# Tokens laid over partitions by chunk in a two-layer recurrent, attention and expert kernel

## The reference

```python
xn = layernorm(x)
# layer 0: a recurrence over 16 states, gated, and a small per-feature network
u = LN(xn)@Ws.T + bs + LN(xn)@Wi.T + bi
h_t = tanh(h_{t-1} @ A.T + u_t)                    # over the 2048 tokens
s = (H@Wo.T + bo) * sigmoid(LN(xn)@Wg.T + bg) + xn
t = xn@Win + bin_
g = einsum(relu(t[..., None]*W1 + b1), W2) + b2; g = g@Wout + bout
x = x + s * silu(g)
xn = layernorm(x)
# layer 1: attention over the first axis (the 4 sequences), 16 heads, causal, softmax with 1 + sum
q, k, v = xn@Wq.T + bq, xn@Wk.T + bk, xn@Wv.T + bv
s = attention_one(q, k, v)                         # 4 x 4 scores per token and head
# 8 experts, 2 per token, 2048 places per expert, given out in token order
logits = xn.reshape(8192, 256)@wg
topv, topi = top_k(softmax(logits), 2)
pos = cumsum(one_hot(topi.T)) - 1                  # places; a token past the last place is dropped
g = sum over the 2 of gate * (relu(xn@w1[e] + b1[e])@w2[e] + b2[e])
x = x + s * silu(g)
```

## Time and profile before

| | us |
|---|---|
| median of three runs | 1446.29 (1444.0 to 1450.97) |
| the profiled execution | 1449.93, of which the span in the trace is 1448.0 |
| PE busy | 1192.6 (82%) |
| DVE busy | 1016.9 (70%) |
| ACT busy | 639.6 (44%) |
| POOL busy | 624.9 (43%) |

### The profile page before, as it was taken

One profiled execution on the slowest core, in us unless ns is written; L12 is line 12 of the kernel. 1 busy time (PEld: TensorE's weight loads), 2 busy tenths in 40 slices (PEclk: granted clock), 3 DMA queues, 4 the chain that ended last, 5 costly groups with the idle time before them and its releaser, 6 DMA issues. The chain is left out here.

```text
span 1448.0 us, 23203 instructions
## 1 busy us (share of the span) xinstructions
PE 1192.6 (82%) x7551; PEld 809.2 (56%) x7551; DVE 1016.9 (70%) x1925; ACT 639.6 (44%) x981; POOL 624.9 (43%) x530
## 2 busy tenths in 40 slices
PE   4899999588888886244999989999999998999910
PEld 3566666366666665032665656766666666666610
DVE  7756667658888888595666776676676765776638
ACT  4855555234444432004446354454454454553522
POOL 6500000137777777203545545545445445464430
PEclk9999999699999999556999999999999999999965
DMA  9250000000000010103546445554446545465469
GB/s 323 98 194 1 1 0 1 15 30 30 30 30 30 30 31 16 59 4 103 114 73 130 82 89 115 102 100 82 101 95 111 107 66 121 83 108 106 63 160 344
DMA packets 165458, 122.35 MB, mean 85 GB/s; under 512 B 88528, under 2 KB 158032, under 8 KB 165232
## 3 DMA queue, kind: packets, MB, share of 16 engines
q1 hardware_dynamic: 131424, 83.90, 20.0%
q0 software_dynamic: 25200, 35.85, 16.1%
q10 hardware_dynamic: 8736, 1.33, 0.5%
HBM read 58.91 MB, written 44.30 MB: 71 GB/s over the span
## 5 line engine op out<-in xcount | busy, mean ns | idle before, releaser
L1721 ACT ACTIVATE e_h_all<-e_pH,e_b1c,e_h_scale 128x512 f32<-128x512 f32 x256 | 199.8, 780 | 285.7 <-PE e_pH L1762 262.6
L1776 PE MATMUL e_pY<-e_w_hi,e_h_hi 128*128 128x256 f16 x1024 | 279.6, 273 | 20.4 <-DVE e_w_lo L1596 11.1
L1505 POOL DMA_INDIRECT e_xg<-xn_rows,e_icol x140 | 161.9, 1157 | 284.1 <-DVE e_icol L1537 251.3
L1778 PE MATMUL e_pY<-e_w_hi,e_h_lo 128*128 128x256 f16 x1024 | 279.1, 273 | 0.0
L1777 PE MATMUL e_pY<-e_w_lo,e_h_hi 128*128 128x256 f16 x1024 | 279.1, 273 | 0.0
L1520 POOL DMA_INDIRECT expert_sums<-e_yo,e_dcol x128 | 213.2, 1665 | 81.1 <-issue 43.8
L1639 DVE TENSOR_TENSOR e_h_lo<-e_h_all,e_h_hi 128x512 f16<-128x512 f32 x256 | 177.5, 693 | 62.6 <-ACT e_h_hi L1721 56.4
L1760 PE MATMUL e_pH<-e_xT,e_w_hi 128*128 128x512 f16 x512 | 196.0, 383 | 22.5 <-DMA e_xT<-e_xs 15.4
L1761 PE MATMUL e_pH<-e_xT,e_w_hi 128*128 128x512 f16 x512 | 195.8, 382 | 0.0
L1762 PE MATMUL e_pH<-e_xT,e_w_lo 128*128 128x512 f16 x512 | 195.6, 382 | 0.0
L1776 PEld LDWEIGHTS e_pY<-e_w_hi,e_h_hi 128*128 128x128 f16 x1024 | 100.1, 98 | 46.7 <-DVE e_h_lo L1639 28.1
(11 more groups left out here) (245 smaller groups left out, 2195.5 us busy)
## 6 DMA issues: line engine op xcount, KB each, us to landing
raw<-expert_w SPq DMA_DIRECT2D x18, 1024.0 KB
expert_sums<-a_zero SPq DMA_DIRECT2D x10, 1024.0 KB, 10.7
x_st<-x SPq DMA_DIRECT2D x16, 512.0 KB, 8.9
xn_rows<-c_xn SPq DMA_DIRECT2D x16, 512.0 KB, 3.0
f_ya<-expert_sums SPq DMA_DIRECT2D x16, 512.0 KB, 6.8
out<-f_ya SPq DMA_DIRECT2D x16, 512.0 KB, 5.8
e_xg<-xn_rows,e_icol POOLq DMA_INDIRECT x140
e_xT<-e_xs SPq DMA_TRANSPOSE x136
```

The source lines that it names most:

```text
L1505: pool.indirect_dma_start(xg[:, q, 0:D + E], None, v.xn3_dram, bass.IndirectOffsetOnAxis(icol[u][:, q:q + 1], axis=0), bounds_check=N - 1, ...
L1721: last = act.activation(dst, pH[h % NPH][:, :], ACT.Relu, bias=b1c[eu][:, h:h + 1], scale=h_scale[eu][:, 0:1])
L1776: pe.matmul(pY[:, q, :], h_hi[:, h, cols], w2_hi[:, h, :], start=(h == 0), stop=False)
L1778: last = pe.matmul(pY[:, q, :], h_lo[:, h, cols], w2_hi[:, h, :], start=False, stop=(h == HT - 1))
```

## The change

Tokens are laid over partitions anew. A sequence's 2048 positions are read as (p t) instead of (t p): partition p holds tokens 16 p to 16 p + 15, which is one chunk, and tile t holds token t of every chunk. So step l of the recurrence is tile l: `take_u` writes 128 contiguous numbers, PE reads `h_st` directly, and `states` and its 16 copies are gone. `x_st` is laid out by sequence, then tile, so that a load of four tiles reads runs of 4 KB where it read 1 KB. Rows of the two scratch tensors are in the order (p t b).

`route` scans each partition's one-hot of 1024 first, sums only the 64 row totals with two small matmuls, and adds the base back; its one-hot is laid out by (pick, sequence), expert, tile. The index of a row needs two more operations. `tiles` writes all 16 tiles out. `combine` writes all tiles out too, loads eight tiles ahead, forms the result in `x_st` and stores two tiles at a time, on one semaphore.

```diff
...
+def token_rows(rows):
+
+    return rows.rearrange("(p t) d -> p t d", p=P)
+
+
 def load_x(eng, v, n):

     for b in range(B):
-        rows = v.x[b, n * FIRST * P:(n + 1) * FIRST * P, :]
-        eng.dma_start(v.x_st[:, n * FIRST:(n + 1) * FIRST, b * D:(b + 1) * D],
-                      rows.rearrange("(t p) d -> p t d", p=P)).then_inc(v.x_in[n - 1], 16)
+        eng.dma_start(v.x_st[:, b, n * FIRST:(n + 1) * FIRST, :],
+                      token_rows(v.x[b])[:, n * FIRST:(n + 1) * FIRST, :]).then_inc(v.x_in[n - 1], 16)
...
 def tiles(eng, body):
-
-
-    with eng.Fori(0, NT // 2 - 2) as i:
-        for u in range(2):
-            body(i, u, 4)
-    for i in (NT // 2 - 2, NT // 2 - 1):
-        for u in range(2):
-            body(i, u, NT - 1 - 2 * i - u)
+    for t in range(NT):
+        body(t // 2, t % 2, NT - 1 - t)
...
-                    dve.tensor_tensor(v.u_st[:, :, t * CPT:(t + 1) * CPT].rearrange("p l c -> p c l"),
-                                      src[:, 0:P].rearrange("p (c l) -> p c l", l=L),
-                                      ag[:, :].rearrange("p (c l) -> p c l", l=L), ALU.mult).then_inc(u_evac, 1)
+                    dve.tensor_tensor(v.u_st[:, t, :], src[:, 0:P], ag[:, :], ALU.mult).then_inc(u_evac, 1)
...
-                def states(t, u, reused=True):
-
-                    if reused:
-                        act.wait_ge(o_done, t - 1)
-                        act.sem_inc(passed, 1)
-                    act.activation(hs[u][:, :, :], v.h_st[:, :, bass.ts(t, CPT)].rearrange("p l c -> p c l"),
-                                   ACT.Copy).then_inc(hs_ready, 1)
...
-                states(0, 0, reused=False)
-                states(1, 1, reused=False)
                 normalise(0, 0, 0)
                 take(xnT, pT, t_done, t_evac, 0)
-                states(2, 0)
                 normalise(1, 1, 0)
...
-                def output(t, u):
-                    pe.wait_ge(hs_ready, t + 1)
+                def output(t):
                     for n in range(2):
                         half = slice(2 * GRP * n, 2 * GRP * n + 2 * GRP)
                         last = pe.matmul(pX[:, 2 * n:2 * n + 2, :].rearrange("p b d -> p (b d)"),
-                                         hs[u][half, :, :].rearrange("p c l -> p (c l)"),
+                                         v.h_st[half, :, :][:, t, :],
                                          v.wo_pad[half, 2 * n:2 * n + 2, :].rearrange("p b d -> p (b d)"),
...
-                    ins = dve.tensor_tensor(hot[:, k, :, :], expert, each(first[:, k, :]), ALU.is_equal)
-                    ins.then_inc(hot_ready, 1)
-                    dve.wait_ge(hot_ready, k + 1)
+                    linked(dve.tensor_tensor(one_hot(k), by_tile(expert), by_tile(each(first[:, k, :])), ALU.is_equal))
                     if k == 0:
-                        linked(dve.scalar_tensor_tensor(lg2[:, :, :], hot[:, 0, :, :], -1e30, lg, ALU.mult, ALU.add))
-
+                        linked(dve.tensor_tensor(eq[:, :, :], expert, each(first[:, 0, :]), ALU.is_equal))
+                        linked(dve.scalar_tensor_tensor(lg2[:, :, :], eq[:, :, :], -1e30, lg, ALU.mult, ALU.add))
+
+                linked(dve.tensor_tensor_scan(pos[:, :, :, :].rearrange("p n e t -> p (n e t)"),
+                                              within[:, :, :, :].rearrange("p n e t -> p (n e t)"),
+                                              hot[:, :, :, :].rearrange("p n e t -> p (n e t)"),
+                                              0.0, ALU.mult, ALU.add))
+                linked(dve.tensor_copy(rows[:, :, :], pos[:, :, :, NT - 1]))
+                dve.sem_inc(rows_ready, 1)
                 dve.wait_ge(counts, 1)
-                dve.tensor_copy(total[:, :, 0:NG], ptot[:, 0, :].rearrange("p (g e) -> p e g", e=E))
-                dve.wait_ge(counts, 2)
-                linked(dve.tensor_copy(total[:, :, NG:K2], ptot[:, 1, :].rearrange("p (g e) -> p e g", e=E)))
+                linked(dve.tensor_copy(total[:, :, :], ptot[:, 0:KB * E].rearrange("p (n e) -> p e n", e=E)))
                 linked(dve.tensor_tensor_scan(before[:, :, :].rearrange("p e n -> p (e n)"),
-                                              within[:, :, :].rearrange("p e n -> p (e n)"),
+                                              within2[:, :, :].rearrange("p e n -> p (e n)"),
                                               total[:, :, :].rearrange("p e n -> p (e n)"), 0.0, ALU.mult, ALU.add))
-                for k in range(TOPK):
-                    linked(dve.tensor_tensor(pos[:, k, :, :], pin[:, k, :].rearrange("p (g e) -> p g e", e=E),
-                                             before[:, :, k * NG:(k + 1) * NG].rearrange("p e g -> p g e"), ALU.add))
+                linked(dve.scalar_tensor_tensor(base[:, :, :], pin[:, 0:KB * E].rearrange("p (n e) -> p n e", e=E), -1.0,
+                                                before[:, :, :].rearrange("p e n -> p n e"), ALU.add, ALU.add))
+                linked(dve.tensor_tensor(pos[:, :, :, :], pos[:, :, :, :],
+                                         base[:, :, :].unsqueeze(3).broadcast_to([P, KB, E, NT]), ALU.add))
                 linked(dve.tensor_tensor(pos[:, :, :, :], pos[:, :, :, :], hot[:, :, :, :], ALU.mult))
-                linked(dve.tensor_reduce(loc[:, :], pos[:, :, :, :].rearrange("p k g e -> p (k g) e"), AX.X, ALU.add))
+                linked(dve.tensor_reduce(loc[:, :].rearrange("p (n t) -> p n t", t=NT),
+                                         pos[:, :, :, :].rearrange("p n e t -> p n t e"), AX.X, ALU.add))
...
-                dve.tensor_scalar(v.idx[:, 0:P], bits, 16, N - 1, ALU.logical_shift_right, ALU.bitwise_and)
+                dve.tensor_scalar(v.idx[:, 0:P], bits, 16, P - 1, ALU.logical_shift_right, ALU.bitwise_and)
+                linked(dve.tensor_scalar(found[:, :], bits, 23, NG - 1, ALU.logical_shift_right, ALU.bitwise_and))
+                linked(dve.scalar_tensor_tensor(v.idx[:, 0:P], v.idx[:, 0:P], float(NG), found[:, :], ALU.mult, ALU.add))
...
-                for k in range(TOPK):
-                    pe.wait_ge(hot_ready, k + 1)
-                    oh = hot[:, k, :, :].rearrange("p g e -> p (g e)")
-                    pe.matmul(pin[:, k, :], v.cst[:, C_UP:C_UP + P], oh, start=True, stop=True)
-                    pe.matmul(ptot[:, k, :], v.ones, oh, start=True, stop=True).then_inc(counts, 1)
+                pe.wait_ge(rows_ready, 1)
+                flat = rows[:, :, :].rearrange("p n e -> p (n e)")
+                pe.matmul(pin[:, 0:KB * E], v.cst[:, C_UP:C_UP + P], flat, start=True, stop=True)
+                pe.matmul(ptot[:, 0:KB * E], v.ones, flat, start=True, stop=True).then_inc(counts, 1)
...
-                for n in range(NB):
-                    body(i, n, NB)
-            for n in range(NB):
-                body(NT // NB - 1, n, NB - 1 - n)
+        o_out = sem("f_o_out")
 
         with nc.Block() as block:
             @block.sync
             def _(sp):
-                for n in range(NB):
-                    sp.sem_inc(o_out[n], 16)
-                dst = v.out.rearrange("b (t p) d -> t p b d", p=P)
-                rows = v.y_dram[0:N, :].rearrange("(b t p) d -> t p b d", b=B, p=P)
-
-                def load(t, n):
-                    sp.dma_start(ya[n][:, :].rearrange("p (b d) -> p b d", b=B), rows[t]).then_inc(y_in[n], 16)
-
-                for n in range(AHEAD):
-                    load(n, n)
-
-                def body(i, n, left):
-                    t = NB * i + n
+                dst = v.out.rearrange("b (p t) d -> p b t d", p=P)
+                rows = v.y_dram[0:N, :].rearrange("(p t b) d -> t p b d", b=B, p=P)
+
+                def load(t):
+                    sp.dma_start(ya[t % NB][:, :, :], rows[t]).then_inc(y_in[t % NB], 16)
+
+                for t in range(NB):
+                    load(t)
+                for t in range(NT):
                     sp.wait_ge(o_ready, t + 1)
-                    sp.dma_start(dst[t], ya[n][:, :].rearrange("p (b d) -> p b d", b=B)).then_inc(o_out[n], 16)
-                    if left >= AHEAD:
-
-                        m = (n + AHEAD) % NB
-                        sp.wait_ge(o_out[m], 16 * (i + (n + AHEAD) // NB) + 16)
-                        load(t + AHEAD, m)
-
-                rounds(sp, body)
-                for n in range(NB):
-                    sp.wait_ge(o_out[n], 16 * (NT // NB) + 16)
+                    if t + NB < NT:
+                        load(t + NB)
+                    if t % 2:
+                        ts = slice(t - 1, t + 1)
+                        sp.dma_start(dst[:, :, ts, :], v.x_st[:, :, ts, :]).then_inc(o_out, 16)
+                sp.wait_ge(o_out, 16 * (NT // 2))
...
+                for t in range(NT):
+                    y = ya[t % NB]
+                    act.wait_ge(y_in[t % NB], 16 * (t // NB + 1))
+                    act.activation(y[:, :, :], y[:, :, :], ACT.Silu).then_inc(silu_ready, 1)
...
```

(28 more changed lines are left out.)

74 lines of the change are left out of this document (33 added, 41 removed).

## The result

The changed kernel takes 1431.4 us (median of four runs, 1429.75 to 1433.34); beside it the kernel before took 1447.3. The ratio is 0.9889, 95% interval 0.9869 to 0.9908: 16 us less, 13 to 19 by the interval. The forecast was 1426. The profiled execution took 1429.75 us with a span of 1427.9, against 1449.93 and 1448.0.

A forecast was written before the change was run, and what follows sets the result against it. Experts were taken as PE-bound; in attention neither PE nor DVE was full, and loop rounds with table loads cost 16.7 us. Terms summed to -19.9: 1430.0 against the profiled 1449.9, or 1426 against the median 1446.3; range 1415 to 1438.

The forecast's parts named there:

- The six loads and their 16.7: Attention: unrolling turns six ACT table loads into one and saves 16.7 us, bounds 8.5 and 16.7.
- My split of the 3.0 per round into 1.42 of wait and the rest from the clock: Attention: a load adds 1.42 us of PE wait; c_pY and other matmuls at low clock make up the rest.
- the dear tile once in each round: Attention: the timeline was read as one tile of 19.94 us per loop round, with a cheap one between.
- Why 16.93 is the floor: Attention: tiles under 16.94 us not expected, since DVE needs 15.5 per tile plus 0.96 of wait for Exp.
- The copies of h, -0.4: Attention: of ACT's 16 c_hs copies only the first, ahead of PE's first matmul, shows, saving 0.42 us.
- take_u, -1.0: First phase: contiguous writes take 0.29 us instead of 0.388; 1.0 us saved, bounds 0 and 1.6.
- The start, +0.3: Program start: x loads in 4 KB runs share queues with the raw weights; 0.3 us more, bounds 0 and +1.
- Routing, -0.5: Routing: new scan order saves 1.8 us, strided accesses cost 1.3; net 0.5 saved, bounds -1.8 and +1.
- the two adds of the earlier trace: Routing before: two strided adds take 2.07 us for 1024 against 2 x 0.69 contiguous, pricing strides at 0.67 more per 1024.
- Combine, -1.6: Combine: table load ahead of the wait -1.3 us, shorter product-to-sum link -1.6, larger last store +1.3; sum -1.6.
- Experts, 0: Experts: gathered and scattered rows lie further apart, no change expected, bounds -3 and +3 us; slower-gathers rival has chance 0.06.

The follow-up runs named there:

- experiment 1: Kernel before, with ACT's queue of attention alone written out for all 16 tiles, other engines' loops and state copies kept: 1431.8 us, ratio 0.9900.
- experiment 2: Changed kernel with ACT's queue of attention alone put back into the loop of six rounds: 1445.8 us, ratio 0.9983.
- experiment 3: Changed kernel with three small ACT copies ahead of put_logits in six tiles, no table load there: 1447.1 us, ratio 0.9999.
- experiment 6: Changed kernel with ACT's attention queue in the loop and put_logits ahead of the q and k copies: 1427.3 us, ratio 0.9817.
- experiment 5: Changed kernel with put_logits moved ahead of the copies of q and k in ACT's queue: 1419.5 us, ratio 0.9817.
- experiment 7: Changed kernel with combine as before (loop, f_ya, six tiles ahead, store per tile, pass-counting instruction): 1434.3 us, ratio 0.9906.
- experiment 4: Changed kernel with one small ACT copy ahead of put_logits in six tiles, no table load there: 1436.8 us, ratio 0.9915.
- experiment 8: Changed kernel with the second four loads of x held back until the raw weights have landed: 1429.8 us, ratio 0.9879.
- experiment 10: Changed kernel with put_logits ahead of the q and k copies and the second x loads behind the raw weights: 1419.7 us, ratio 0.9810.

## Why the prediction was right, and where it was off

- **The six loads and their 16.7.** Right, to 0.2: 16.48 in the trace. Cause and mechanism are shown by experiments 1 and 2 (the order of one queue brings and takes it), 3 (other work of that length in that place does the same) and 6 (the loads in another place cost nothing). My split of the 3.0 per round into 1.42 of wait and the rest from the clock also holds: 18.35 with the wait alone, 20.0 with both. Not foreseen is that the fall of the clock comes in some tiles and not in others with the same wait; the trace of before had one such tile (421.7 to 440.05, 18.35), which I overlooked when I read "the dear tile once in each round".
- **Why 16.93 is the floor.** I argued it with DVE's lack of room. That was wrong as a floor: DVE is busy 218.21 of the 253 us, and PE's wait for put_logits sets the period, which experiment 5 brought down to 16.27. DVE's own pace, about 16.1 by the estimate there, is the next limit.
- **The copies of h, -0.4.** Right in size. PE's first matmul of attention started 0.44 after DVE's first memset of the stage (269.61 against 269.17) and now starts 0.09 ahead of it (269.76 against 269.85), so 0.53 are gained at the head of the stage.
- **take_u, -1.0.** The operation is as fast as costed (0.29), and the steady part of the pass gains nothing by it: PE's turns start 2.55 apart before and after, and ACT has no idle time there.

```profile
42.00:47.00 5.00, 3.77 (x64) 2.90 (x64) 4.86 (x22) 5.00 (x9) 4.53 (x9) 1.00 0.00 0
```

  ACT is busy 5.00 of 5.00. I had both engines at 97 and 98% in the earlier trace rows and shared the gain out between them. The 0.5 that the pass did gain comes in tiles 2 to 6, whose turns on PE start 2.38 to 2.57 apart where it was 2.55 to 2.67; after them it is 2.55 as before. That gain isn't steady: the other ten traces of the new layout have 48.15 to 48.77 for the pass, experiment 1 with the old one 48.78.
- **The start, +0.3.** The term was mis-sized: +1.28, beyond my upper bound of 1.0. From the landing of the raw weights on, the start is as it was (5.77 from DVE's first operation on them to the statistics, 5.75 before); what grew is DVE's wait for them, 1.80 for 0.51. I had looked at the sizes of the transfers and not at how fast they are issued; whether the issue is the cause isn't shown.
- **Routing, -0.5.** 0.0. Every piece came in near its price, dear ones as well: the strided one-hot 1.01, the wait for PE 1.26, the strided sum 1.86.

```profile
580.80 1.01 DVE L1279 TENSOR_TENSOR d_hot<-cst,d_first 128x512 f32<-128x512 f32 x1
...
591.27 0.23 DVE L1291 COPY d_total<-d_ptot 128x64 f32<-128x64 f32 x1 [1.26 <-PE d_ptot L1342]
...
594.68 1.86 DVE L1300 TENSOR_REDUCE d_loc<-d_pos 128x128 f32<-128x1024 f32 x1
```

  From the second one-hot to the places it takes 9.1 (587.43 to 596.54) where I had 8.9 with the strides, the memsets add 0.4 where I had 0.2, and that is nearly all of the missing 0.5. The strides cost what the two adds of the earlier trace rows said: 1.01 for 512 elements instead of 0.69, 1.86 for 1024 instead of 1.22. The Trainium skill ("SBUF — State Buffer", Specifications) states a penalty for each access that crosses to a new 16-byte line; these rows agree with it.
- **Combine, -1.6.** 1.8 in the trace, 1.9 by experiment 7, from the terms that were named. From SP's first load to the first product it takes 5.07 where it was 6.25 (-1.18, the load out of the wait), from there to the last sum 37.19 for 38.97 (-1.78, the link, 0.11 a tile), and from the start of the last sum to the end 5.85 for 4.70 (+1.15, the larger store).
- **Experts, 0.** The stage's length is as it was within its scatter, but a small cost of the wider spacing of gathered rows isn't excluded. PE's wait for e_xT in the changed kernel:

```profile
L1761 PE MATMUL e_pH<-e_xT,e_w_hi 128*128 128x512 f16 x512 | 195.1, 381 | 26.5 <-DMA e_xT<-e_xs 17.6
```

  It is 17.6 against the 15.4 of the earlier trace rows. Experiment 1, with the old layout, has 15.3, and the ten other traces with the new one have 15.8 to 22.5, so the wait did grow, by 0.4 to 7 us in all. The stage took 747.8 and 750.0 in the two traces with the old layout, and 746.9 to 751.4 in eight with the new one (755.6 to 756.7 in the three beside which the kernel before took 1452): the 1.65 of the first comparison lies inside that, and so would a cost of one or two us.
- **The total.** By the profiled pair the sum was right to 0.3 us (1430.0 against 1429.75). The median of 1431.4 lies 5 us above the 1426. One to one and a half of them is the kernel before, whose median over more runs is 1447.3 to 1448.0 and not 1446.3. The rest is that 20.1 us of the profiled pair are 16 by the medians, and its cause isn't shown. The experts' stage can give some of it: without its 1.65 the other terms give -18.5, inside the interval of -13 to -19. And the profiled execution of before may not be a typical one. Of the 28 executions of it beside experiments 1 to 5, 7, 8 and 10, ten with a mean granted clock of 0.931 to 0.933 took 1442.0 to 1445.8, and eighteen with 0.925 to 0.930 took 1446.7 to 1451.7; the profiled one had 0.928. The 7.7 us that PE's matmuls lost in attention are 15.4 us at half clock, which is 0.005 of the mean over the program (an estimate), the size of that gap. So in some executions the falls of the clock may not have come, and there was less to gain; none of the faster ones has a trace.

## What to carry to other kernels

Look at what stands behind a stall in the same queue, not at its length: 1.28 us of table load cost 2.8 where PE waited behind it and nothing where it didn't. In a loop's body look at the head, where the compiler put such loads in all three kernels here with ACT's attention in a loop and where a consumer may be waiting. And when an engine idles next to the one that waits, ask of each copy in the queue between them whether it could have gone earlier; the logits here had been ready for 10 us.

## What the runs showed of the hardware

The granted clock of TensorE fell from 2.4 to 1.2 GHz for a few us (0.50 in the window of the earlier trace rows) after some waits of PE in attention and not after others: after five of six waits of 2.62, three of six of 2.65, two of six of 1.75, and after none of the waits of 1.20 or 0.54 between the second and the fifteenth c_k copy. Each fall cost about 1.6 us. What decides it between two tiles with the same wait was not found. The kernel before and experiment 2, whose tiles start within 0.3 us of each other, spare the same one of their six. But these counts are of one execution each: the ten of experiment 2 are three of 1441.6 to 1442.2 us with a mean clock of 0.933 or 0.934 and seven of 1445.3 to 1448.3 with 0.926 to 0.928, so the number of falls may change from one execution to the next.
